# A gated cross-attention layer with routed experts: the attention steps of each engine in one list a batch, and the keys spread by ACT

## The reference

```python
x = x + tanh(g_xattn) * xattn(layernorm(x), ctx, mask)
x = x + tanh(g_ffn) * ffn(layernorm(x))

# xattn: 16 heads of 16
Q, K, V = heads(q @ Wq.T + bq), heads(ctx @ Wk.T + bk), heads(ctx @ Wv.T + bv)
energy = where(mask == 0, -1e10, Q @ K.T / sqrt(16))
return (softmax(energy) @ V) @ Wfc.T + bfc

# ffn: 8 experts, each token goes to its best 2
w, idx = top_k(x @ gate, 2);  p = softmax(w)
return sum over the 2 of  p * ((silu(x @ w0[e]) * (x @ w1[e])) @ wo[e])
```

## Time and profile before

| | us |
|---|---|
| median of 3 runs | 1369.81 |
| lowest and highest | 1364.96, 1369.87 |
| the profiled execution, its own time | 1363.92 |
| its span, first to last instruction | 1362.3 |
| PE busy | 1263.6 (93%) |
| DVE busy | 746.4 (55%) |
| ACT busy | 699.2 (51%) |
| POOL busy | 750.6 (55%) |

### The profile page before, as it was taken

One profiled execution on the slowest core, in us unless ns is written; L12 is line 12 of the kernel. 1 busy time (PEld: TensorE's weight loads), 2 busy tenths in 40 slices (PEclk: granted clock), 3 DMA queues, 4 the chain that ended last, 5 costly groups with the idle time before them and its releaser, 6 DMA issues.

```text
span 1362.3 us, 37316 instructions
## 1 busy us (share of the span) xinstructions
PE 1263.6 (93%) x10466; PEld 1109.6 (81%) x10467; DVE 746.4 (55%) x2524; ACT 699.2 (51%) x1780; POOL 750.6 (55%) x1197
## 2 busy tenths in 40 slices
PE   4999999999999999997099999999999999999996
PEld 3888888888888888886078888888888888888885
DVE  5788788877888878873333333333333333333332
ACT  2777677767777777774033333333333333333332
POOL 3367777776777767775434444444444444444443
PEclk9999899989999999996589999999999999999998
DMA  5034333323334333326468863333333333333332
GB/s 157 23 119 138 132 126 123 127 74 116 128 124 136 132 126 128 124 100 218 150 186 213 218 146 53 54 54 54 53 52 53 54 54 54 54 54 50 57 53 34
DMA packets 73976, 139.73 MB, mean 103 GB/s; under 512 B 11604, under 2 KB 55156, under 8 KB 71764
## 3 DMA queue, kind: packets, MB, share of 16 engines
q0 software_dynamic: 32064, 52.46, 19.7%
q1 hardware_dynamic: 39840, 86.05, 19.5%
q10 hardware_dynamic: 2036, 0.75, 0.2%
HBM read 68.95 MB, written 70.27 MB: 102 GB/s over the span
## 4 chain that ended last, share of the span: by engine, by line
PE 49%; issue 1%; DMA 0%; POOL 0%; POOLq 0%; ACT 0%
PE banks L1424 28%; PE psB L1443 14%; PE psT L1432 4%; PE psG L1409 2%; DMA out_dram<-ey,eid 0%; POOL w_part L500 0%; DMA et<-routed_rows 0%; POOL routed_rows L494 0%; POOL out_dram L551 0%; POOLq L545 0%; ACT ey L774 0%; ACT etT L756 0%; POOLq L546 0%; POOLq L306 0%; POOLq L559 0%
## 5 line engine op out<-in xcount | busy, mean ns | idle before, releaser
L1424 PE MATMUL banks<-w_all,etT 128*128 x1620 | 433.3, 403 | 0.7 <-ACT etT L756 0.7
L1424 PEld LDWEIGHTS banks<-w_all,etT 128*128 128x128 f32 x1620 | 286.3, 189 | 51.4 <-issue 3.6
L1151 DVE TENSOR_TENSOR hgT<-psT,hgT 128x512 fp32r<-128x512 f32 x135 | 93.3, 691 | 426.0 <-ACT hgT L768 426.0
L551 POOL DMA_INDIRECT out_dram<-ey,eid x135 | 216.5, 1604 | 91.4 <-issue 48.0
L546 POOL DMA_DIRECT2D et<-routed_rows x135 | 76.8, 569 | 300.6 <-issue 233.0
L1443 PEld LDWEIGHTS psB<-w_all,hgT 128*128 128x128 f32 x1620 | 208.5, 188 | 18.8 <-issue 1.3
L1443 PE MATMUL psB<-w_all,hgT 128*128 x1620 | 218.5, 284 | 0.8 <-ACT hgT L768 0.8
L774 ACT ACTIVATE ey<-psB,ewt 128x256 f32<-128x256 f32 x135 | 64.2, 475 | 234.1 <-PE psB L1443 143.8
L1279 PEld LDWEIGHTS psB<-vbd,probT 128*128 128x128 f32 x1280 | 163.1, 194 | 21.9 <-ACT probT L622 20.1
L1279 PE MATMUL psB<-vbd,probT 128*128 128x51 f32 x1280 | 168.0, 271 | 13.4 <-ACT probT L622 13.4
L762 ACT ACTIVATE hs<-banks 128x512 f32<-128x512 f32 x135 | 80.7, 598 | 185.3 <-PE psT L1432 183.4
(11 more groups left out here) (162 smaller groups left out, 2188.6 us busy)
## 6 DMA issues: line engine op xcount, KB each, us to landing
split_weights<-w_part SPq DMA_DIRECT2D x16, 1536.0 KB, 6.2
w_all<-split_weights SPq DMA_DIRECT2D x32, 768.0 KB, 4.7
et<-routed_rows POOLq DMA_DIRECT2D x135, 129.0 KB, 2.4
xb<-in_x_dram SPq DMA_DIRECT2D x32, 256.0 KB, 2.8
w_raw<-in_L_ffn_w_kernel_dram SPq DMA_DIRECT2D x32, 256.0 KB
out_dram<-x SPq DMA_DIRECT2D x64, 128.0 KB
w_raw<-in_L_ffn_wo_kernel_dram SPq DMA_DIRECT2D x16, 256.0 KB
cb<-in_ctx_dram SPq DMA_DIRECT2D x32, 77.0 KB
```

The source lines that it names most:

```text
L551: gp.indirect_dma_start(out=out, out_offset=bass.IndirectOffsetOnAxis(ap=eid[:, u:u + 1], axis=0), in_=ey[:, u % 2, :], in_offset=None, co ...
L1151: dve.tensor_tensor(hgT[:, 1].rearrange("p c q -> p (c q)"), psT[:], hgT[:, 0].rearrange("p c q -> p (c q)").bitcast(F32), ALU.subtract).t ...
L1424: m = pe.matmul(banks4[:, bank], etT[:, u % 2, a, c], weight(e, c, w, n), start=(j == 0), stop=(j == len(steps) - 1))
```

## The change

The function `batch` of PE, ACT, DVE and POOL no longer loops over t. It is one list for both tiles, each with an order of its own. SP's is as it was. POOL's `spread_keys` loses its two multiplications and is called `mask_keys`. ACT gets a `spread_keys` that makes the same kbd with two instructions (one for each head of a pair, high and low parts together), each a copy with the scale own2, 0 or 1 for each partition. Waits on semaphores keep their meaning; nothing else is computed in another way.

```diff
-            def spread_keys(b, u):
-
+            def mask_keys(b, u):
 
                 after(gp, *([(s_ps, RG * QT * (b - 1))] if known(b, 2) else []))
                 gp.tensor_copy(mrow[:, u], masked[:, bass.ds(b * K2, K2)]).then_inc(mrow_done, 1)
-                gp.wait_ge(k_sb, b + 1)
-                for a in range(2):
-                    gp.tensor_tensor(kbd[:, u, a], kT2[:, a].bitcast(F32).rearrange("p c (o k) -> p c o k", o=1).to_broadcast([P, DC, HP, K2]),
-                                     own2[:].rearrange("p (o s l) -> p o s l", o=1, l=1).to_broadcast([P, DC, HP, K2]), ALU.mult).then_inc(kbd_done, 1)
...
             def batch(b, u, n):
...
+                i, u4 = b * QT, u * QT
+                if known(i, 2):
+                    rstd_2(i - 2)
+                if known(b, 2):
+                    number_rows(i - 4, u4)
+                for q, r in ((n - 1, 1), (n - 1, 2)) if u == 0 else ((n, 0),):
+                    if known(q, 0):
+                        split_low(q, r)
+                if known(b, 2):
+                    weigh(b - 2, u)
+                    number_rows(i - 3, u4 + 1)
+                if more:
+                    mask_keys(b + 1, 1 - u)
+                if more2:
+                    rstd_1(b + 2)
+                if known(i + 1, 2):
+                    rstd_2(i - 1)
+                if known(b, 2):
+                    scatter(i - 4, u4, b - 2)
+                    scatter(i - 3, u4 + 1, b - 2)
+                if more:
+                    residual(b + 1, 1 - u, n + u)
...
+            def spread_keys(b, u):
+
+                act.wait_ge(k_sb, b + 1)
+                if known(b, 2):
+                    act.wait_ge(s_ps, RG * QT * (b - 1))
+                for s in range(HP):
+                    act.activation(kbd[:, u, :, :, s].rearrange("p a c k -> p (a c) k"), kT2[:].bitcast(F32).rearrange("p a c k -> p (a c) k"), ACT.Copy,
+                                   scale=own2[:, s:s + 1]).then_inc(kbd_done, 1)
...
+            act.wait_ge(dv_const, 2)
+            spread_keys(0, 0)
             v_first(0)
...
+                i, u4 = b * QT, u * QT
+                if known(i, 3):
+                    exp_gap(i - 3, 1, b - 2)
+                if known(i, 1):
+                    o_evac(i - 1)
+                if known(i, 2):
+                    norm_2(i - 2, 0, (u4 - 2) % 4, n if u4 >= 2 else n - 1)
+                t_evac(i, 1)
+                if known(i, 2):
+                    copy_row(i - 2, (u4 - 2) % 4)
+                if more:
+                    q_evac(b + 1, 1 - u)
+                t_evac(i, 2)
+                if known(i, 2):
+                    n2_evac(i - 2)
+                exp_scores(i + 1, 1)
+                if known(i, 2):
+                    gated_evac(i - 2)
+                if more:
+                    spread_keys(b + 1, 1 - u)
+                    v_first(b + 1)
+                t_evac(i + 1, 0)
...
+                if known(i + 1, 1):
+                    o_evac(i)
+                t_evac(i + 1, 1)
+                if known(i + 1, 2):
+                    norm_2(i - 1, 1, (u4 - 1) % 4, n if u4 + 1 >= 2 else n - 1)
...
+                o_norm(i, 0)
+                if known(i, 1):
+                    residual_1(i - 1, 1 - u, 1, b - 1)
+                o_norm(i, 1)
+                if known(i, 1):
+                    stats_2(i - 1, 1, 0)
+                if known(i + 1, 4):
+                    free_rows(i - 3, 0)
+                if known(i + 1, 2):
+                    stats_2(i - 1, 1, 1)
...
+                if more:
+                    v_split(b + 1, 0)
...
+                if more:
+                    s_largest(i + 2, 0, 1)
+                    s_largest(i + 2, 0, 0)
...
+                if more:
+                    v_split(b + 1, 2)
+                    s_shift(i + 2, 0)
...
+                if more:
+                    s_negate(i + 2, 0)
+                    v_evac(b + 1, 1 - u)
+                o_norm(i + 1, 0)
...
+                if known(i + 1, 1):
+                    residual_1(i, u, 0, b)
+                o_norm(i + 1, 1)
+                if known(i + 1, 1):
+                    stats_2(i, 0, 0)
...
+                if known(i, 1):
+                    o_T(i - 1)
+                if more:
+                    queries(b + 1, 0)
+                prob_T(i, 0, 1)
+                if more:
+                    queries(b + 1, 1)
+                    pe.wait_ge(k_raw, DC * (b + 2))
+                attend(i, u, b, 0)
+                prob_T(i, 0, 2)
+                if known(i, 2):
+                    n2_T(i - 2, (u4 - 2) % 4)
+                attend(i, u, b, 1)
+                attend(i, u, b, 2)
+                if known(i, 1):
+                    project(i - 1)
+                if known(i, 2):
+                    gate(i - 2)
...
+                if more:
+                    values(b + 1)
+                prob_T(i + 1, 1, 0)
+                if more2:
+                    pe.wait_ge(o_sb, i + 1)
+                    ctx_T(b + 2, u, n + 1)
+                if known(i + 1, 1):
+                    o_T(i)
+                if more:
+                    scores(i + 2, 1 - u, 0, b + 1)
+                prob_T(i + 1, 1, 1)
+                if more2:
+                    pe.wait_ge(ctxT_sb, b + 3)
+                attend(i + 1, u, b, 0)
+                prob_T(i + 1, 1, 2)
+                attend(i + 1, u, b, 1)
+                if known(i + 1, 2):
+                    n2_T(i - 1, (u4 - 1) % 4)
+                if more:
+                    flatten_values(b + 1)
...
+                    project(i)
+                if more2:
...
+                if more:
+                    scores(i + 3, 1 - u, 1, b + 1)
+                if more2:
+                    pe.wait_ge(o_sb, i + 2)
+                    keys(b + 2)
+                if more:
+                    prob_T(i + 2, 0, 0)
```

## The result

| | before | after |
|---|---|---|
| median, us | 1367.67 (4 runs) | 1306.76 (4 runs) |
| lowest and highest | 1364.96, 1369.87 | 1306.42, 1307.04 |
| span of the profiled execution | 1362.3 | 1305.2 |

The ratio is 0.9555, with a 95% interval of 0.9532 to 0.9578. The forecast was 1317 us, a ratio of 0.961, and a range of 1303 to 1345. Ratios are of the fast executions alone: two of the ten of e2b_keys_only took 1891 and 2443 us and are not in its ratio.

The account below looks back on a forecast made before the run. PE was taken to bound the kernel. The pace's 28 x (18.59 - 17.4) = 33.3 us, clock falls 11.5 and tail 2.0 made 46.8 off the profiled 1363.92, so 1317 us; range 1303 to 1345.

Parts of the forecast that it names:

- The bound: In the attention loop PE is busy for 508.3 of 532.0 us, so only its waits and low clock can be won.
- the three waits: PE waits around n2_T and attend, 0.27, 0.69 and 0.35 us, since POOL's shift reaches ACT late; all 1.31 a batch won.
- The pace: Attention loop, 28 batches: 18.59 us a batch falls to 17.4, which is 17.28 of PE's own work plus 0.13.
- the new waits: PE's new order costs 0.08 us at the second tile's transposes and 0.05 before flatten_values, 0.13 a batch.
- The range: 1303 to 1345 us, leaving out one in ten at both ends; low end pace 17.1, high end 18.0 with all falls.
- POOL's room: POOL's shift comes at about +0.4 in the batch, norm_2 is due on ACT at about 1.4; some 2 us of room.
- Keys on ACT: Two copies of about 0.46 us, 0.9 a batch, lie in a hole between the gate's eviction and v_first, hidden.
- The clock's falls: Falls of PE's clock in the loop, right behind the waits that go, were taken as gone: 11.5 us won.
- The rival of falls in the row of transposes: More transposes in a row on PE lower the clock in most batches, up to 1424 us; chance 0.05.
- Prologue and tail: Prologue 0, within 1 us; tail, 82.1 us before, 2 us won, from 0 to 3, as expert fetches start earlier.
- DVE doesn't set the pace: Rival: DVE sets the loop's pace, 18.0 us a batch, with half of the clock falls staying, 1339 us; chance 0.17.
- Nothing stayed, neither waits nor falls: Two rivals: waits go but clock falls stay, 1323 to 1329 us, chance 0.15; nothing moves, within 7 of 1366, chance 0.05.

Follow-up runs that it names:

- e2b_keys_only: The kernel before with only the key spreading moved from POOL to ACT, all other lists as before; ratio 1.0011 to the kernel before.
- e1b: The kernel after with the keys spread by POOL again, in the group where the kernel before took 1364.89 us; 1317.41 us, ratio 0.9645.
- r_before: The kernel before, unchanged, run and profiled again beside the follow-up kernels; 1369.93 us in one run.
- A: The one group of follow-up runs in which the kernel before took 1364.89 us (1361.77 to 1370.39), the level of the main result.
- e1: The kernel after with the keys spread by POOL again, in a group where the kernel before took about 1404 us; 1475.1 us, ratio 1.0503.
- B: The four groups of follow-up runs in which the unchanged kernel before took 1404.1 to 1405.1 us.
- r_after: The kernel after, unchanged, run and profiled again beside the follow-up kernels; 1305.79 us, ratio 0.956.

## Why the prediction was right, and where not

**The bound, the three waits and their reason**: right. PE bound the loop, and the waits of 0.27, 0.69 and 0.35 went together with ACT's wait for the shift. e1b is the counter-test: put POOL's work back, and the wait for the shift is back, at 0.76 a batch. That the clock falls behind the waits that went away is borne out too, by all eleven falls of the two profiles of the kernel before.

**The pace**: the mechanism right, the size off. This is nearly the whole error. The loop's 28 batches were to take 17.4 us each and took 17.05, which makes 28 x 0.35 = 9.8 of the 10 us between 1317 and 1306.8. The step that failed reads "its own work stays 18.59 - 1.31 = 17.28": it counted PE's small waits as work, of which the prediction itself named "about 0.3 us" and left them where they were. PE of the kernel before, then of the kernel after:

```profile
273.86 0.64 PE L1210 MATMUL psA<-ident,xn 128*128 128x128 f32 x4
274.43 0.63 PE L1267 MATMUL psT<-ident,prob 128*128 128x128 f32 x4
274.99 0.32 PE L1246 MATMUL banks<-mrow,share 32*128 32x308 bf16 x4
```

```profile
268.93 0.60 PE L1254 MATMUL psA<-ident,xn 128*128 128x128 f32 x4
269.37 0.17 PE L1362 MATMUL psT<-chosen_any,upper 128*128 128x8 bf16 x1
```

Four transposes cost 0.57 and 0.56 before and 0.44 bare. Summing the bare price of each group gives an estimate of 16.75 us a batch (16.7 where the smallest price of each group is taken). Before, 18.59 - 16.75 - 1.31 = 0.53 was lost in small pieces, and after only 17.05 - 16.75 = 0.30, the new waits included. So 0.53 - (0.30 - 0.05) = 0.28 more was won than counted, and the new waits cost some 0.05 and not 0.13: 265.71 - 265.44 = 0.27 for two transposes of 0.23 in the second tile, and none before flatten. A sum over bare prices would have shown that there was 0.53 to win beside the 1.31. What ended these small pieces wasn't tested: PE's own order changed along with the other lists.

**The range**: the time fell into it by luck. The pace of 17.05 lies outside of the paces that the range was drawn from, 17.1 to 18.0. By the prediction's own terms the low end is 1363.9 - (41.7 + 11.5 + 2) = 1308.7 us and not 1303, and 1306.76 lies between the two; the high end, 28 x 0.59 + 2 = 18.5 us won, does give 1345.

**POOL's room**: wrong, without consequence. The shift was to come at +0.4 after the opening o_T with some 2 us of room. It came at 256.12 - 255.16 = +0.96, with ACT's norm_2 at +1.28 (due at 1.4): room of 0.3. e1b shows how little it is, as 1.35 us more on POOL made 0.76 of wait. The count took scatters and residual to end at 14.8 of the batch; rstd_2 starts right behind the residual (ended at 254.54, started at 254.62), so POOL has no idle time there.

**Keys on ACT**: hidden, as said; in size 0.546 us each against 0.46 taken, inside the bounds of 0.41 and 1.01. From the groups from 200 to 500 us:

```profile
L677 ACT ACTIVATE kbd<-kT,own 128x308 fp32r<-128x308 f32 x34 | 16.9, 546 | 0.0
```

The Trainium skill (ScalarE: Activation LUTs, What ACT_TABLE_LOAD costs) gave an estimate of 0.54, and the trace agrees with it better than with the line between two copies: the scale held in a tensor is what a plain copy doesn't have. They end at 262.92, and v_first starts at 262.81, as neighbours on ACT overlap a little. The values were done at 262.51 (PE, 261.44 + 1.07); in e1b v_first starts 0.04 behind that point. So the keys hold v_first up by some 0.26 us, and the hole is shorter than they are; flatten on PE doesn't start later for it.

**The clock's falls**: gone, 11.5 us, as taken. The 5.9 us between the profiled execution and the median, put down to less than two falls, fit r_before too: three falls more, 4.8 us. In A the clock is 1.00 also in e1b, which has 0.36 us more a batch, but there the longest idle time of PE is 0.4 between 66 and 530 us, and no half-microsecond is as empty as the one of the earlier trace rows: PE works for 0.12 us in the emptiest, where the kernel before has one with 0.02 to 0.06 in nearly every batch. Behind the gap of 2.35 in e1 the clock is at 0.50. The rival of falls in the row of transposes found no support: that stretch stands in each batch and the clock is 1.00.

**Prologue and tail**: 2 us predicted for the tail, 1.7 measured (82.1 to 80.4); for the prologue 0 within 1, measured 1.9 (69.62 to 67.74), outside of that bound. The expert stage is 1 us longer.

**The rivals.** DVE doesn't set the pace: it is busy for 14.74 us of 17.05. Nothing stayed, neither waits nor falls. The rival on the slow side, falls in the row of transposes, didn't come. B shows another way to be slow that nobody had listed: PE's report for the flattened values comes 3.3 us late, DVE's `v_evac` waits for it, PE waits 2.35 for DVE, and then the clock is lower. Nothing in the profile of the kernel before in A points to it.

## What to carry to other kernels

When PE bounds a loop, sum the bare price of every group of matmuls and take the pace from that: here small waits went away along with the large ones, though no run separates why. Work that is moved to the engine with a hole is worth what it frees on the engine it left, at the place where others wait for it (here 1.35 us on POOL, 0.36 us a batch). And measure a tight schedule in more than one group of runs, beside the old kernel: this one is 4.5% faster where the old one takes 1365 us, and close relatives of it are 5 to 6% slower where the old one takes 1404.

## What the runs showed of the hardware

**POOL holds up DVE for a whole instruction.** POOL and DVE of e1b at one place:

```profile
296.50 1.27 POOL L499 TENSOR_TENSOR w_part<-w_raw,w_part 128x512 fp32r<-128x512 f32 x1
296.53 1.41 DVE L901 TENSOR_TENSOR kT<-kT 128x154 fp32r<-128x154 f32 x1
```

The subtraction of kT takes 0.31 us by itself (median of 32: 318 ns) and 1.41 when it starts 0.03 behind POOL's split: it ends 0.17 behind it. In the kernel after the same split meets a 16-element product, which takes 0.94 in place of 0.16. The Trainium skill (SBUF — State Buffer, SBUF: two separate sides) says that DVE with two inputs in SBUF and POOL lock a shared port for a full instruction, and the trace agrees. This too came with the keys' move: DVE is busy for 447.68 us of 495.40 in e1b and for 427.95 in r_after, although it does more batches there. What it is worth in PE's time wasn't measured.

**Small operations tell who is in the way.** From 200 to 500 us, in the kernel before and then after:

```profile
L976 DVE TENSOR_TENSOR chosen<-expert_f,topf 128x16 f32<-128x16 f32 x31 | 15.5, 500 | 0.0
```

```profile
L998 DVE TENSOR_TENSOR chosen<-expert_f,topf 128x16 f32<-128x16 f32 x35 | 5.6, 160 | 0.0
```

These are means. After, each takes 0.16 us. Before, half of them do too; the others meet POOL's split and take 0.41 or 1.23, as here in r_before:

```profile
283.45 1.27 POOL L500 TENSOR_TENSOR w_part<-w_raw,w_part 128x512 fp32r<-128x512 f32 x1
283.52 1.23 DVE L976 TENSOR_TENSOR chosen<-expert_f,topf 128x16 f32<-128x16 f32 x1
```

So a mean far above the shortest one is time behind POOL that the page counts as busy.

**The same program has two times.** The kernel before took 1365 us in one group and 1404 in four, each level within 0.7%. The ratio of one and the same kernel with keys on POOL was 0.9645 in A and 1.0503 in B. The sign of it is an idle stretch of nearly the same length at the same line, batch after batch, put down to "remote" on the engine that waits for PE, whose semaphore update comes up to 4.05 us behind the end of its matmuls, or to "issue" inside one of PE's own groups. In the profiles at 1365 us there is no such update.
